# Convolution stage: one block of values between the second and third quarter of energies, and two of ten extra matmuls on a zeroed tile kept

## The reference

```
q, k, v = conv1x1(x)                      # q, k: 16 channels, v: 128 channels
energy  = einsum('bci,bcj->bij', q, k)    # viewed as (b, h, w, h', w')
attn    = softmax(energy, axis=-1)        # over w', 16 values at a time
out     = einsum('bchk,bhwkv->bcwv', v, attn)
x       = gamma * out + x
```

## Time and profile before

| | |
|---|---|
| median of 3 runs | 193.51 us (193.37, 193.51, 195.26) |
| profiled execution | 193.34 us |
| its span, first to last instruction | 191.6 us |
| PE busy | 179.9 us, 94% |
| ACT busy | 117.8 us, 62% |
| DVE busy | 100.2 us, 52% |
| POOL busy | 75.2 us, 39% |
| mean granted TensorE clock | 0.995 |

### The profile page before, as it was taken

How to read it: one execution, slowest core, us unless ns; L and a number is a source line. 1 busy time by engine, 2 the same in 40 slices (tenths; PEclk the granted TensorE clock), 3 DMA queues, 4 the chain that set the end, 5 groups by cost and what they waited for, 6 DMA issues and landing times.

```text
span 191.6 us, 3226 instructions
## 1 busy us (share of the span) xinstructions
PE 179.9 (94%) x1274; PEld 118.4 (62%) x1274; DVE 100.2 (52%) x172; ACT 117.8 (62%) x176; POOL 75.2 (39%) x63
## 2 busy tenths in 40 slices
PE   6999999899899999998998999899999999999991
PEld 3269768476456654445463556366666888888880
DVE  1569333778094356566000700070528979976673
ACT  3525833126626632224986498635769899999980
POOL 8304219585402020002633263328632939433222
PEclk9999999999999999999999999999999999999998
DMA  4998000000000000570000000000000087000001
GB/s 137 323 339 333 14 0 3 0 0 0 3 5 0 0 2 3 173 261 7 0 0 3 0 0 0 3 0 2 0 0 3 6 242 250 2 0 3 0 0 55
DMA packets 5647, 10.41 MB, mean 54 GB/s; under 512 B 1264, under 2 KB 1648, under 8 KB 5376
## 3 DMA queue, kind: packets, MB, share of 16 engines
q1 hardware_dynamic: 5216, 10.12, 15.3%
q10 hardware_dynamic: 416, 0.08, 0.2%
HBM read 9.65 MB, written 0.56 MB: 53 GB/s over the span
## 4 chain that ended last, share of the span: by engine, by line
PE 80%; issue 5%; DVE 5%; ACT 4%; POOL 3%; DMA 2%; DVEq 0%; POOLq 0%; ACTq 0%
PE PS L1094 10%; PE PS L1074 8%; PE PS L1078 7%; PE PS L1075 7%; PE PS L1102 4%; PE PS L1100 4%; PE PS L1031 4%; PE PS L1099 4%; PE PS L947 4%; DVE nmx L633 3%; PE PS L960 3%; PE PS L860 2%; PE PS L1047 2%; PE PS L849 2%; PE PS L817 2%
## 5 line engine op out<-in xcount | busy, mean ns | idle before, releaser
L473 ACT ACTIVATE room<-PS,b_sb 128x512 f32<-128x512 f32 x64 | 43.6, 687 | 32.6 <-PE PS L1078 31.8
L328 POOL TENSOR_TENSOR x_sb<-x_sb,room 128x512 f32<-128x512 f32 x15 | 22.5, 1503 | 53.1 <-DVE room L721 53.1
L712 DVE TENSOR_TENSOR Gl<-room,Gh 128x512 fp32r<-128x512 f32 x32 | 29.4, 934 | 10.6 <-ACT Gh L422 10.4
L1074 PE MATMUL PS<-x2h,w1h 128*128 128x512 f32 x64 | 32.8, 512 | 2.2 <-ACT room L473 2.2
L1094 PE MATMUL PS<-room,w_sb 128*128 128x512 f32 x64 | 32.1, 593 | 0.0
L633 DVE TENSOR_REDUCE nmx<-PS 128x4 f32<-128x1024 f32 x16 | 19.4, 1225 | 12.1 <-PE PS L960 8.3
L1078 PE MATMUL PS<-x2l,w1h 128*128 128x512 f32 x64 | 25.3, 396 | 0.0
L1075 PE MATMUL PS<-x2h,w1l 128*128 128x512 f32 x64 | 25.2, 394 | 0.0
L652 DVE RECIPROCAL att<-PS 128x256 f32<-128x256 f32 x4 | 7.0, 1757 | 34.0 <-PE PS L1047 34.0
L320 POOL TENSOR_TENSOR pairs<-probs 128x512 f32<-128x512 f32 x12 | 15.0, 1274 | 16.2 <-ACT probs L463 16.2
L1074 PEld LDWEIGHTS PS<-x2h,w1h 128*128 128x128 f32 x64 | 12.0, 188 | 14.7 <-issue 10.9
(11 more groups left out here) (121 smaller groups left out, 265.8 us busy)
## 6 DMA issues: line engine op xcount, KB each, us to landing
room<-comb_rows SPq DMA_DIRECT2D x16, 256.0 KB, 5.5
w1raw<-w SPq DMA_DIRECT2D x8, 256.0 KB, 5.7
w_sb<-w SPq DMA_DIRECT2D x2, 1024.0 KB, 10.6
x_sb<-x SPq DMA_DIRECT2D x2, 256.0 KB, 3.3
out<-x_sb SPq DMA_DIRECT2D x2, 256.0 KB, 4.3
attw_sb<-attw SPq DMA_DIRECT2D x1, 320.0 KB, 5.3
cst<-consts SPq DMA_DIRECT2D x1, 228.5 KB, 5.0
convw_sb<-convw ACTq DMA_DIRECT2D x1, 80.0 KB, 3.3
```

The source lines that it names most:

```text
L328: nc.gpsimd.tensor_tensor(t2[:, cols(p)], t2[:, cols(p)], part[:, s, :], ALU.add).then_inc(acc_done, 1)
L473: nc.scalar.activation(G[:, n % GR, :], PS[:, U_BANK[n % 2], :], ACT.Gelu, bias=b1_sb[:, c:c + 1])\
L712: nc.vector.tensor_tensor(Gl[:, n % GR, :], G[:, n % GR, :], Gh[:, n % GR, :].bitcast(f32), ALU.subtract)\
L1074: mm(o, w1h[e][:, ms], x2h[:, cols(p)], start=True, stop=False)
```

## The change

The program of PE in the convolution stage gets another order. `conv_values(0)` comes between `energy(1)` and `energy(2)`. Of the ten turns behind the projections, eight go: the one ahead of `conv_bias`, those behind the quarters 1, 2 and 3 of the energies, the one in each `conv_values`, and both ahead of `conv_apply(0)`. The one behind `energy(0)` and the one between the applications stay. On ACT `conv_values_out(0)` comes ahead of `conv_exp(2)` instead of behind it; `conv_values_out(1)` stays behind `conv_exp(3)`. DVE, POOL and SP keep their programs.

```diff
@@ ScalarE
             conv_exp(0)
             conv_exp(1)
             high_weights(0)
+            conv_values_out(0)
             conv_exp(2)
-            conv_values_out(0)
             conv_exp(3)
             conv_values_out(1)
@@ TensorE, conv_values(i)
                 for k in range(4 * i, 4 * i + 4):
                     last = mm(PS[:, 4 + i, (k % 4) * C:(k % 4 + 1) * C], x_k[:, k, :], convw_sb[:, QK:QK + C],
                               start=False, stop=True, skip_group_check=True)
-                    if k % 4 == 1:
-                        turn(1)
                 last.then_inc(vT_done, 1)
@@ TensorE, the order
-            turn(1)
             for i in range(2):
                 conv_bias(i)
-            for q in range(WQ):
-                energy(q)
-                turn(1)
-            for i in range(2):
-                conv_values(i)
-            turn(2)
+            energy(0)
+            turn(1)
+            energy(1)
+            conv_values(0)
+            energy(2)
+            energy(3)
+            conv_values(1)
             conv_apply(0)
             turn(1, 0)
             conv_apply(1)
```

## The result

The changed kernel is slower, by less than 1%. Its median is 195.06 us (194.82 to 196.22, 4 executions) against 193.44 us before (193.18 to 195.26), a ratio of 1.0084 with a 95% interval of 1.0046 to 1.0122. Eleven more executions in the experiments gave 195.70 us and a ratio of 1.0108 (1.0075 to 1.0142). The forecast was 192.9 us; rival A had named 195.0.

A forecast was written before the change was run, and what follows sets the result against it. PE was taken to bound the convolution stage, with DVE's softmax nearly equal. Of 2.2 us on PE's own clock, waits left 0.44: 193.34 - 0.44 = 192.9 us, forecast 192.5 to 193.1, range 192.3 to 195.0.

The forecast's parts named there:

- rival A: PE's new pause ahead of the first application drops the clock; one application takes 2.07 us more, 195.0 us; chance 0.2.
- give nothing: Removing the two turns ahead of the application gains nothing, since they run while PE waits for ACT's copy anyway.
- the granted clock at 1.00 from 19 to 25 us: Sign expected in the profile after: the full 2.4 GHz on PE through the applications.
- The pause itself: PE stands still ahead of the first application from 17.93 to 19.81 us, 1.9 us.
- Gain before the clock: First application on PE starts at 19.81 us instead of 20.25, a gain of 0.44 us carried to the end.
- The bias: On PE behind the projections, it begins 0.43 us sooner without its turn, takes 1.72 us and ends at 9.46 us.
- The values: Eight records on PE ahead of quarter 2 take 1.78 us plus 0.22 for an exposed weight load.
- DVE's wait for quarter 2: DVE waits 0.70 us for energy(2), ready at 14.98 us, 0.27 us later than before.
- The copy: ACT's conv_values_out(1) is held by its place behind conv_exp(3), starts at 19.16 us and takes 0.61 us.
- The scaled quarters: Inputs of the applications: POOL's quarter 1 at 18.46 us and DVE's quarter 3 at 21.26 us, both in time.
- Rival B: Behind the convolution stage, waits on DVE, ACT and POOL take up the gain: 193.3 us; chance 0.15.
- C: energy(2) on PE is in time because weight loads overlap, so DVE keeps its head start: gain 1.1, 192.3 us; chance 0.1.

The follow-up runs named there:

- two turns in the pause: Changed kernel with the two turns ahead of the first application put back: median 193.35 us, ratio 0.9992 to the kernel before.
- copy first: Changed kernel with ACT's copy of the second values ahead of the exponential of quarter 3: median 194.46 us, ratio 0.9985 to the kernel before.
- order of before, copy first: Kernel before without most turns, ACT's copy of the second values ahead of quarter 3's exponential, one turn ahead of the first application: 191.87 us, ratio 0.9917.
- shortest chain: Changed kernel with energy 2 ahead of values 0, ACT's second copy ahead of quarter 3's exponential, one turn ahead of the first application: 194.50 us, ratio 0.9989.
- no turn behind energy 0: Changed kernel without its turn behind energy(0) and with four turns ahead of the first application: median 192.71 us, ratio 0.9957 to the kernel before.
- four turns in the pause: Changed kernel with four turns ahead of the first application: median 193.43 us, ratio 0.9978 to the kernel before.

## Why the prediction was wrong

**The step that failed** is the clock: the prediction wrote that the two turns ahead of the application "give nothing" when they go, expected the granted clock at 1.00 from 19 to 25 us, and gave rival A, the fall in the new hole, only 0.2. The clock fell to 0.50 at 20.8 us, which cost 1.54 us in the two applications and the turn between them, and it fell in 15 of 15 executions. The pause itself was sized well (1.96 us for 1.9). What it was weighed against was misread. The 1.24 us that it took for a pause survived at L633 are the length of DVE's instruction; PE stood still there for 0.74 us, as the row says from which it was taken (busy 1.26 of 2 us), and the longest pause of PE in mid-kernel of that trace is 0.89 us. So the new pause was twice what had been survived, not half as long again. And one profiled execution that survives a pause is weak evidence, because executions of one program differ.

Rival A had the mechanism and the place right, and its 0.2 should have been the larger share. That its 195.0 lies so close to 194.8 is partly luck: it took a gain of 0.44 that was 0.10, and a whole application doubled, 2.07 us, where 1.54 us were lost; the two errors cancel for the most part.

**Gain before the clock: 0.10 us instead of 0.44.** Even without the fall the forecast would have been missed. Two terms were mis-sized; the first shows what a turn covers.
- The bias took 1.91 us from the end of the projections, where 1.72 was carried over. With the turn the two took 0.43 + 1.72 = 2.15, so dropping it gave 0.24, not 0.43: the bias's first weight load had lain under the turn. The text saw this effect for the values and not here.
- The values took 2.10 instead of 2.00 us. With both, quarter 2 reached DVE at 15.28 us, not 14.98. The last 0.04 us of the difference lie in small steps on DVE and ACT behind it.

**What held.** DVE's wait for quarter 2 was forecast at 0.70 us and was 0.71. The copy stood behind `conv_exp(3)` and was what PE waited for. The scaled quarters were in time. At the full clock the changed kernel would stand near 193.2 us, as it does with two turns in the pause (193.25): no change against 193.4. Rival B did not happen: the 1.44 us at L585 arrive whole at the end. C did not happen either: `energy(2)` was late, as the row of 1.78 us for eight records had said.

**The turns ahead of the application** were priced at nothing because PE waited there anyway. That was right for the chain and wrong for the kernel: put back, they are worth 1.7 us or more. The rule of the Trainium skill cited for A (TensorE: Matmul & The Clock Gate, section "HAM oscillation — how this bites in real kernels"), that a wait between bursts of matmuls drops the clock and the next burst begins slow, gave the right sign, though the waits of its example are longer than the one here. The trace agrees with one difference: the application began at the full clock and lost it 0.65 us later.

**By part:** the order alone costs 0.3 us; the turns alone bring 0.95 us where the fall costs nothing and cost 0.6 in the median; both together bring about 0.15 at the full clock and cost 1.6 to 2.2 as run. The parts do not add up, because the slack of 0.62 us that hid part of the order's delay is there only as long as the turns are.

**Open.** The clock also fell while PE was busy, at 13.6 us (copy first), 14.0 (order of before, copy first), 16.2 (shortest chain), 16.5 (no turn behind energy 0), 16.8 (four turns in the pause) and 17.6 us (two turns). All have few turns among the energies and values, but no run changed that alone and showed a difference. A rival to the pause as such stands for the same reason: a turn in the pause both shortens it and adds work, and no kernel had those turns elsewhere with the pause left as it was. What is shown is that without the turns there the clock falls, not which of the two properties holds it.

## What to carry to other kernels

A filler matmul in a pause is not free to remove. Here it paid to put fillers where the engine waits and to take them out where they lie on the chain: with the old order that gave 192.47 us, against 193.47 before and 195.06 for the changed kernel. A fall of the clock cost nothing where it lay under the values and cost 0.8 to 0.9 of its own time again where an application or energies lay wholly under it, so what stands behind a block of fillers matters; no run moved a fall on purpose. Judge such a change by the spread of many executions with their granted clock, not by one profile, and look at the clock of the good executions too.

## What the runs showed of the hardware

- A granted clock of 0.50 makes two neighbouring quarters of energies 1.9 times as long (3.57 against 1.88 us) and a first application that lies wholly under it 1.8 times (3.79 and 3.80 against 2.07 us), but 16 records of 128 columns with full float32 weights take 4.09 us at 0.50 for most of their length and 4.08 at 1.00.
- At 0.50 the weight load of an application takes 326 ns instead of 187, that of the values 335 instead of 334.
- The clock fell in stretches in which every window has PE busy for its whole length (13 to 14 us in the copy-first kernel, 17 to 18 us with two turns in the pause).
- A pause of PE of 1.4 us went with a fall in 12 of 12 executions and one of 2.0 us in 15 of 15.
- The same program meets a fall in some executions and not in others: above 194.2 us in 24 of 104 for the kernel before.
